# Six products instead of eight in the first two convolutions of images 2 and 3, with the extra filter mixes made on GpSimd

## The reference, cut to what matters

```python
y_sam = relu(bn(conv3x3(x, w_sam)));  s = spatial_attention(y_sam)   # softmax over 256 pixels, per image
y_cam = relu(bn(conv3x3(x, w_cam)));  c = channel_attention(y_cam)   # softmax over 128 channels
x1 = conv3x3(concat(s, c), w_out)                                    # 256 -> 128 channels
# then masked bottleneck + coordinate attention, two attention blocks with concepts, a last attention
```

## Time and profile before

| | us |
|---|---|
| median of 3 runs | 115.08 (114.97 to 115.64) |
| the profiled execution | 114.44 |
| its span, first to last instruction | 112.7 |
| PE busy in the span | 105.7 (94%) |
| DVE, ACT, POOL busy | 79.6, 51.1, 16.8 |

### The profile page before, as it was taken

How to read it: one execution, slowest core, us unless ns; L and a number is a source line. 1 busy time by engine, 2 the same in 40 slices (tenths; PEclk the granted TensorE clock), 3 DMA queues, 4 the chain that set the end, 5 groups by cost and what they waited for, 6 DMA issues and landing times.

```text
span 112.7 us, 2152 instructions
## 1 busy us (share of the span) xinstructions
PE 105.7 (94%) x769; PEld 89.4 (79%) x769; DVE 79.6 (71%) x250; ACT 51.1 (45%) x148; POOL 16.8 (15%) x28
## 2 busy tenths in 40 slices
PE   5999989989999999989998899998999999999991
PEld 5988869858868979989996657696789998677571
DVE  1669557578899796975986444759564786688871
ACT  5151676987333243030112503014785637768760
POOL 5007996000000000000000000003300003333000
PEclk9999999999999999999999999999999999999999
DMA  3999910000000000000000000000000000000112
GB/s 78 280 370 395 435 73 6 0 0 0 3 0 0 0 3 6 0 0 0 6 0 0 0 6 0 3 0 0 0 6 0 0 0 0 0 6 0 47 53 87
DMA packets 3321, 5.24 MB, mean 47 GB/s; under 512 B 496, under 2 KB 2928, under 8 KB 3184
## 3 DMA queue, kind: packets, MB, share of 16 engines
q1 hardware_dynamic: 3168, 5.11, 13.0%
q10 hardware_dynamic: 144, 0.01, 0.1%
HBM read 4.59 MB, written 0.52 MB: 45 GB/s over the span
## 4 chain that ended last, share of the span: by engine, by line
PE 72%; DVE 13%; ACT 10%; issue 2%; DVEq 0%; ACTq 0%
PE psum L1026 11%; PE psum L1044 9%; PE psum L1110 8%; PE psum L1376 4%; PE psum L1350 4%; PE psum L1368 3%; PE psum L1151 3%; PE psum L1421 2%; PE psum L1434 2%; PE psum L1343 2%; DVE eo L658 2%; PE psum L1454 2%; PE psum L1188 2%; PE psum L1301 2%; PE psum L1358 2%
## 5 line engine op out<-in xcount | busy, mean ns | idle before, releaser
L1110 PE MATMUL psum<-spin 128*128 128x256 f32 x58 | 10.2, 330 | 1.2 <-DVE spin L582 1.2
L355 POOL TENSOR_TENSOR att_s<-xc,x 128x256 f32<-128x256 f32 x3 | 2.2, 725 | 59.5 <-DVE xc L898 59.5
L1110 PEld LDWEIGHTS psum<-spin 128*128 128x128 f32 x58 | 8.9, 228 | 1.5 <-DVE spin L582 1.2
L361 POOL TENSOR_SCALAR att_c<-x,gbv 128x256 f32<-128x256 f32 x4 | 3.8, 961 | 19.3 <-DVE x L947 19.3
L1026 PE MATMUL psum<-mixed_x,w_mix_cam 128*128 128x256 f32 x24 | 6.4, 384 | 0.0
L1026 PE MATMUL psum<-mixed_x,w_raw_cam 128*128 128x256 f32 x24 | 6.2, 379 | 0.0
L1044 PE MATMUL psum<-mixed_s,w_mix_out_s 128*128 128x128 f32 x48 | 6.2, 275 | 0.0
L1044 PEld LDWEIGHTS psum<-mixed_s,w_mix_out_s 128*128 128x128 f32 x48 | 5.9, 192 | 0.1
L1026 PE MATMUL psum<-mixed_x,w_raw_sam 128*128 128x256 f32 x24 | 5.7, 382 | 0.0
L1044 PE MATMUL psum<-mixed_c,w_mix_out_c 128*128 128x128 f32 x48 | 5.7, 275 | 0.0
L1044 PEld LDWEIGHTS psum<-mixed_c,w_mix_out_c 128*128 128x128 f32 x48 | 5.5, 192 | 0.0
(11 more groups left out here) (249 smaller groups left out, 266.3 us busy)
## 6 DMA issues: line engine op xcount, KB each, us to landing
par<-in_late SPq DMA_DIRECT2D x1, 1422.0 KB, 7.8
wide_x<-in_x SPq DMA_DIRECT2D x2, 288.0 KB, 3.9
w_raw_sam<-in_w_sam SPq DMA_DIRECT2D x3, 192.0 KB, 3.1
w_raw_cam<-in_w_cam SPq DMA_DIRECT2D x3, 192.0 KB, 4.9
w_raw_out_s<-in_w_out SPq DMA_DIRECT2D x3, 192.0 KB, 5.0
w_raw_out_c<-in_w_out SPq DMA_DIRECT2D x3, 192.0 KB, 4.9
out<-y SPq DMA_DIRECT2D x2, 128.0 KB, 1.7
out<-y SPq DMA_DIRECT2D x4, 64.0 KB, 1.5
```

The costliest lines, as they stand in the source:

```text
L361: nc.gpsimd.tensor_scalar(x3b[:, b, :], x3[:, b, :], gbv[:, 0:1], None, ALU.add).then_inc(ev["f_xb"], 1)
L1110: mm(bank[k][:, 0:HW], spin[:, 0:P], spin[:, :], start=True, stop=True, skip_group_check=True)
```

## The change

Images 2 and 3 of `sam` and `cam` go over to four from six; images 0 and 1 stay with two from four. For that:

- `sam_second` has 18 matmuls of 128 columns in place of 12 of 256, and runs as one piece before `qk(0)`; `cam` is split into `cam_first` (12) and `cam_second` (18), in the same places as before, two or four of the smaller matmuls where one or two of the larger stood.
- DVE mixes the columns of images 2 and 3 of x with `mix_columns_six`, and that helper is rewritten for x, s and c: four differences (`f, e, c, h`, 128 elements each) become one difference of columns two apart (512 elements, `mix_t`), of which every fourth element is then read.
- POOL makes the second filter mixes for `sam` and `cam` too: its list is now two-mix `sam`, mix `cam`, two-mix `cam`, mix `out_s`, two-mix `out_s` (15 operations in place of 9). ACT scales the `sam` filters before the square root and the `cam` filters before `take_inner("sam", 0)`.
- `join_six` is split into `join_six_inner` (six DVE operations) and `join_six_outer` (two), used for `sam`, `cam` and out. `relu_in` for images 2 and 3 now writes pixels in order.

The first piece is from POOL's list, the second from ACT's behind `load_table(ACT.Sqrt)`, the next from DVE's and the last from PE's.

```diff
+            mix_weights_two("sam")
+            mix_weights("cam")
+            mix_weights_two("cam")
+            mix_weights("out_s")
+            mix_weights_two("out_s")
...
+            scale_weights("sam")
             act.wait_ge(ev["bn_var"], 1)
...
             dve.wait_ge(d_x[1], 16)
-            mix_columns("x", 1, INNER_FIRST, ev["x_mix"])
+            mix_columns_six("x", 1)
...
                 nc.vector.scalar_tensor_tensor(four(a), at[2], -4.0, at[4], ALU.mult, ALU.add).then_inc(diff, 1)
                 nc.vector.scalar_tensor_tensor(four(b), at[1], -4.0, at[3], ALU.mult, ALU.add).then_inc(diff, 1)
-                nc.vector.tensor_tensor(four(c), at[4], at[2], ALU.subtract).then_inc(diff, 1)
-                nc.vector.tensor_tensor(four(e), at[3], at[1], ALU.subtract).then_inc(diff, 1)
-                dve.wait_ge(diff, 6 * i + 2)
+                dve.wait_ge(diff, before + 2)
                 nc.vector.tensor_tensor(to(1), images(a), images(b), ALU.add).then_inc(done, 1)
                 nc.vector.tensor_tensor(to(2), images(a), images(b), ALU.subtract).then_inc(done, 1)
...
+                nc.vector.tensor_tensor(t[:, :].rearrange("p (r w) -> p r w", w=W), d[:, :, 2:2 + W], d[:, :, 0:W],
+                                        ALU.subtract).then_inc(diff, 1)
+                dve.wait_ge(diff, before + 3)
+                nc.vector.scalar_tensor_tensor(to(3), tk[1], 2.0, tk[2], ALU.mult, ALU.add).then_inc(done, 1)
+                nc.vector.scalar_tensor_tensor(to(4), tk[1], -2.0, tk[2], ALU.mult, ALU.add).then_inc(done, 1)
+                nc.vector.scalar_tensor_tensor(to(0), tk[0], -4.0, tk[2], ALU.mult, ALU.add).then_inc(done, 1)
+                nc.vector.scalar_tensor_tensor(to(5), tk[1], -4.0, tk[3], ALU.mult, ALU.add).then_inc(done, 1)
...
-            join_inner("sam", 1, bank[2])
+            join_six_inner("sam", 1, bank[2], eo[:, 1, :, :], 2, ev["sam_y"])
             qk_low(0)
             qk_low(1)
-            join_outer("sam", 1, bank[3], eo[:, 1, :, :], ev["sam_y"])
+            join_six_outer("sam", 1, bank[3], eo[:, 1, :, :], ev["sam_y"])
...
-            sam_second(0, 8)
+            sam_second(0, 18)
             pe.wait_ge(d_early, 16)
             qk(0)
             qk(1)
-            sam_second(8, 12)
+            cam_first(0, 2)
             s_score(0)
             s_score(1)
-            cam(0, 2)
+            cam_first(2, 4)
```

More of the change, by code:

```diff
@@ L330, in _, with mix_weights @@
             nc.gpsimd.memset(hpad[:, :, :], 0.0).then_inc(ev["zeroed"], 1)
-            for n in ("cam", "out_s"):
+            def mix_weights(n):
                 done = ev[f"{n}_w"]
@@ L373, in _, with scale_weights @@
             load_table(ACT.Sqrt)
+            def scale_weights(n):
+                for k, (i, factor) in enumerate(((0, 0.5), (2, 2.0))):
+                    act.wait_ge(d_w[n][i], 16)
+                    nc.scalar.mul(w_mix[n][:, 2 + k, :], w_raw[n][:, i, :], factor).then_inc(ev["scaled"], 1)
+            scale_weights("sam")
             act.wait_ge(ev["bn_var"], 1)
@@ L429, in _ @@
             nc.scalar.copy(ident_r[:, :], ident).then_inc(ev["ident_r"], 1)
[L430 to L434, removed]
+            scale_weights("cam")
             take_inner("sam", 0, bank[0])
@@ L602, in mix_columns_six @@
                 images = lambda t: t.rearrange("p (b s) -> p b s", b=2)
-                to = lambda k: mixed[n][:, k, 2 * i:2 * i + 2, 1:1 + H, :].rearrange("p b r j -> p b (r j)")
-                diff, done = ev[f"{n}_diff"], ev[f"{n}_mix"]
-                if i:
+                t = mix_t[n]
+                tk = [t[:, k:2 * H * W:4].rearrange("p (b s) -> p b s", b=2) for k in range(4)]
+                to = lambda k: mixed[n][:, k, first:first + 2, 1:1 + H, :].rearrange("p b r j -> p b (r j)")
+                first = 0 if n == "x" else 2 * i
+                diff, done = ev["mix_diff"], ev[f"{n}_mix"]
+                before = 3 * [("x", 1), ("s", 0), ("s", 1), ("c", 0), ("c", 1)].index((n, i))
+                if i and n != "x":
                     dve.wait_ge(done, 6)
@@ L654, in join_outer, with join_inner @@
-            def join_outer(n, i, o, out_map, done):
-                dve.wait_ge(ev[f"{n}_outer"], i + 1)
[L656 to L659, removed]
+            def join_inner(n, o):
+                dve.wait_ge(ev[f"{n}_m1"], 1)
+                nc.vector.tensor_tensor(pq[:, 0, 0, :], o[:, HW:2 * HW], m1_sb[:, 0, :],
+                                        ALU.add).then_inc(ev[f"{n}_pq"], 1)
+                nc.vector.tensor_tensor(pq[:, 0, 1, :], m1_sb[:, 0, :], o[:, HW:2 * HW],
+                                        ALU.subtract).then_inc(ev[f"{n}_pq"], 1)
@@ new lines, in join_six_outer @@
+            def join_six_outer(n, i, o, to, done):
+                before = 2 * SIX_JOINS.index((n, i))
+                dve.wait_ge(ev[f"{n}_outer"], i + 1)
+                dve.wait_ge(ev["join_last"], before + 1)
+                nc.vector.scalar_tensor_tensor(phase(to, 0), o[:, 0:HALF], 0.25, last[:, i, 0, :], ALU.mult,
+                                               ALU.add).then_inc(done, 1)
+                dve.wait_ge(ev["join_last"], before + 2)
+                nc.vector.scalar_tensor_tensor(phase(to, 3), o[:, HALF:HW], 1.0, last[:, i, 1, :], ALU.mult,
+                                               ALU.add).then_inc(done, 1)
@@ L756, in _ @@
             s_residual(0)
-            join_inner("cam", 0, bank[2])
+            join_inner("cam", bank[2])
             s_residual(1)
@@ L766, in _ @@
             c_max(0)
-            join_inner("cam", 1, bank[2])
+            join_six_inner("cam", 1, bank[2], eo[:, 1, :, :], 2, ev["cam_y"])
             c_norm(0)
-            join_outer("cam", 1, bank[3], eo[:, 1, :, :], ev["cam_y"])
+            join_six_outer("cam", 1, bank[3], eo[:, 1, :, :], ev["cam_y"])
             mix_weights("out_c")
@@ L1012, in _, with conv @@
             mm = nc.tensor.matmul
-            def conv(n, half, k, o_inner, o_outer, order, k0=0, k_last=None):
-                src = "x"
+            def conv(n, k, o_inner, o_outer, order):
                 i, dy = order[k // 3], k % 3
@@ L1044, in conv_six @@
                 return mm(o[:, c:c + HALF].rearrange("p (b s) -> p b s", b=2), w[:, C * dy:C * (dy + 1)],
-                          mixed[src][:, i, 2 * half:2 * half + 2, dy:dy + H, :].rearrange("p b h j -> p b (h j)"),
-                          start=(n == "out_s" and dy == 0 and c == 0), stop=(n == "out_c" and dy == 2),
+                          mixed[src][:, i, b:b + 2, dy:dy + H, :].rearrange("p b h j -> p b (h j)"),
+                          start=(first and dy == 0 and c == 0), stop=(final and dy == 2),
                           skip_group_check=True)
```

203 lines of the change are left out of this document (102 added, 101 removed).

## The result

The changed kernel takes 122.09 us (median of 4 runs, 121.71 to 123.66), the kernel before 115.03 beside it: ratio 1.0605 (95% interval 1.0524 to 1.0686). The profiled execution took 121.96 us with a span of 120.2, against 114.44 and 112.7. The medians take in executions that lie more than 1.5% above the fastest of their kernel, such as the fourth here (123.66, at a lower granted clock); the ratios leave them out.

What follows compares the result with a forecast made beforehand. Early on, DVE and POOL taking turns on SBUF, not PE, were taken to bound the kernel: second relu +7.3, less 0.2, less 0.6 later, +6.5 us, median 121.5. Range 116.6 to 123.8; the main case's own 119.5 to 123.5.

Steps and rivals of the forecast that it cites:

- The bound: PE is busy 94%, but from 10 to 25 us DVE and ACT are also in the chain; PE's 2.4 us may not count.
- What POOL does: From 7.7 us, POOL mixes and two-operand DVE operations alternate; waits sum to about 6.9 us, DVE free at 18.2, not 10.6.
- my walk: DVE's and POOL's queues stepped through from 7.7 us: bn_inv waits to 8.54, to(3) starts at 14.53, to(5) at 17.88.
- The third rival: DVE's column mixes: DVE keeps its turn, POOL enters only when DVE waits for its own result; +2.5, 117.5 us; 20%.
- the second: Rival for DVE's column mixes: no collision beyond what is there, DVE free at 11.3, total about 114.6 us; 9%.
- Under ACT's queue: join_six_inner, 20.9 to 23.1 us: one step caught for 0.7, hidden under ACT; kst ends at 24.45, second relu +7.3.
- Given back: From the second relu on: 0.2 us from its in-order writes, then 0.6 from cam_second and shorter column mixes, carried to the end.
- Sum: Whole kernel: 7.1 - 0.6 = +6.5 us, giving 120.9 for the profiled execution and 121.5 for the median.
- The clock: Rival for PE's gaps up to 24.5 us: clock falls to 1.2 GHz, +3 us more, 124.5; 4%.
- ACT's copies: Scaling after the Sqrt load needs no table load; otherwise a 1.28 us load before it and one after, before 8.1 us.

Runs made afterwards that it cites:

- e6: Changed kernel with POOL's nine mixes for sam and cam replaced by memsets of about the same length, filters constant; 115.29 us, ratio 1.0037.
- e7: Changed kernel with c_norm(0) between the second cam join's first two and last four operations, and c_turned(0) before the relu on ACT; 122.17 us, ratio 1.0613.
- e9: Kernel before with six products only in cam's second half, column mixes spread, POOL's mixes held back, changed kernel's order around c_norm; 115.78 us, ratio 1.0056.
- e3: Kernel before with six extra POOL additions, three ahead of the cam mixes and three between its filters, written to an unread tile; 117.85 us, ratio 1.0235.
- e1: Changed kernel, but POOL starts its filter mixes only when DVE has finished all ten column mixes of x; 118.35 us, ratio 1.0266.
- e10: Changed kernel run again without edits, for comparison on one chip with c_norm moved ahead of the join's end; 123.31 us, ratio 1.0718.
- e11: Changed kernel with c_norm(0) ahead of the join's last four operations and c_turned(0) before the relu, run again beside the unedited one; 122.37 us, ratio 1.0620.
- e2: Changed kernel with sam's second filter mixes moved from POOL to DVE, POOL starting cam only after the column mixes; 117.82 us, ratio 1.0236.

## Why the prediction was right, point by point

- **The bound.** Right: PE's 94% told nothing of the first 25 us. In e6, with PE's savings and without the collisions ahead of 20 us, the time is that of the kernel before. One reading was wrong without harm: the 24 instructions in 5.22 us are the twelve matmuls of one half of `sam`, not of all images; the 0.435 each is right.
- **What POOL does.** Right in cause, order and near in size. In turn, one each: seven of nine mixes caught. Up to `to(3)` my walk holds within 0.03 us: `bn_inv` and `bn_shift` went free and `bn_tmp` and `a` were caught, where I had it the other way round, with the same sum. I had DVE free at 18.2; it was 17.36, because `to(4)` slipped in. The third rival (DVE keeps its turn) had the first `pq` at about 14; the second had it at 11 to 12.
- **Under ACT's queue.** Wrong. I had one step of `join_six_inner` caught, for 0.7 us, and put it under ACT. Two were caught (0.84 and 1.06 us, against 0.28 alone in e6). ACT had finished `qk_high` at 23.0, DVE came to the first `qk_low` at 23.05: DVE led from there, and `kst` ended at 24.81 where I had 24.45. ACT was 1.0 us earlier than in my sum and `kst` 0.4 later, so that the term is 1.4 us short, and the mix that went free hid 0.8 of it. That the total fits so well is in this part luck. The second relu was +7.8, not +7.3.
- **Given back.** Mis-sized: I had 0.2 for the relu and 0.6 later, together 0.8; it was 0.3. The relu itself took 0.81 us and not 0.87, so 0.06 and not 0.2. The other term that failed is the mix of every fourth element: I took 0.25 us each from between bounds of 0.20 and 0.31, and it is 0.30, so `mix_columns_six` saves nothing (0.00, not 0.2). PE had the channel Gram matrix ready 1.0 us earlier relative to the relu, as forecast, but DVE's s mixes held `c_max` back to 0.7, and `cprob` came only 0.1 earlier and not 0.3. The reason I gave, the join ahead of `c_norm`, and the PE gap of about 1 us were right, and e7 to e9 show it.
- **Sum.** +6.5 forecast, +7.1 in the medians and +7.5 in the profile: both misses had the same sign.
- **The clock.** I gave 4% to a fall that costs 3 us. It occurred in seven of the ten executions of the changed kernel and costs 1.4. The chance was far too low; that it hardly moved the first median, with one such execution of four, is luck. It goes with the spread: 121.7 to 122.2 us at a full clock, 122.8 to 123.9 at the lower mean clock.
- **ACT's copies.** The scaling of `sam`'s filters ran under the table for Sqrt, at 4.20 and 5.67 us for 0.53 and 0.52 us, with no table load between that table's own (1.15) and the square root (6.10).

## What to carry to other kernels

Before moving elementwise work to GpSimd, look at what VectorE does in the same microseconds: here its operations with two SBUF operands, even those of two elements, waited for nearly the whole GpSimd operation in front of them when that one read SBUF, one turn each. Delay GpSimd's list to a stretch in which VectorE reads PSUM, or cut its operations small. And matmul time saved is worth only what the next wait of PE lets through: reorder what feeds that wait first.

## What was not expected of the hardware

- Twelve matmul instructions of `sam`, the first to start behind the zeros, at 4.75 us, took from 2.82 us (before) to 3.99 (e3), at a granted clock that is recorded as full throughout. No run here shows why.
- A `tensor_scalar` on DVE with one tensor operand in SBUF is caught too: in e1 two of them in the first `s_norm` took 1.42 us beside POOL's mixes, 0.62 in the kernel before with POOL idle; in e6 1.70.

```profile
23.47 1.42 DVE L747 TENSOR_SCALAR prob<-prob,rinv 128x256 f32<-128x256 f32 x2
```

- TensorE's granted clock fell behind a gap of 2.0 us in the profiles of e10 and e11 and did not in the first profile of the changed kernel, with a gap of 2.03 us, nor in that of e2, with 2.27. The first profile of e7 does not compare: its gap was 1.47 us.
- Reading every fourth element (stride of 16 bytes) costs 0.30 us for 128 elements on DVE against 0.20 packed, while writing every fourth has a pitch of 0.22 (`eo` at 46.47, the next at 46.69).
